# Gate logits from raw output rows, the norm's scale in the turned copy, two residual products for three, and a new step order

## The reference, cut to what matters

```python
x = L0_attn_x                                    # 4 x 1024 x 256, 4096 rows
x = x + 0.5 * ffn(layernorm(x))                  # 8 experts, capacity 160, top 1
x = x + attn(layernorm(x))
x = x + 0.5 * ffn(layernorm(x))

# attn, after the gated complex scan and the projection Wo:
y   = layer_norm(y + x, ln1_scale, ln1_bias)
h   = gelu(y @ W1 + b1)
out = layer_norm(h @ W2 + b2 + y, ln2_scale, ln2_bias)
# ffn: logits = tokens @ gate_w + gate_b, softmax, argmax, dispatch, two products, combine
```

## Time and profile before

| | us |
|---|---|
| median of 3 runs | 762.57 (762.26 to 764.51) |
| the profiled execution's own time | 763.36 |
| its span | 761.7 |
| first stage, to the first load of `attention` | 0 to 145.2 |
| `attention` | 145.2 to 650.6 |
| second expert stage | 650.6 to 761.7 |

### The profile page before, as it was taken

How to read it: one execution, slowest core, us unless ns; L and a number is a source line. 1 busy time by engine, 2 the same in 40 slices (tenths; PEclk the granted TensorE clock), 3 DMA queues, 4 the chain that set the end, 5 groups by cost and what they waited for, 6 DMA issues and landing times. The chain is left out here.

```text
span 761.7 us, 11459 instructions
## 1 busy us (share of the span) xinstructions
PE 638.8 (84%) x4229; PEld 571.8 (75%) x4229; DVE 465.7 (61%) x1012; ACT 465.5 (61%) x831; POOL 207.8 (27%) x321
## 2 busy tenths in 40 slices
PE   6848999175798999999999999899985995379995
PEld 3437999153577888789789889889885895379994
DVE  5663500235686888988988988978989542631000
ACT  3314443048767898897997988988876352134440
POOL 6140011210121425226235145142231331130112
PEclk9959999678779999999999999999999998579998
DMA  6996970330100201201301211011011130834720
GB/s 196 337 301 210 344 238 24 105 125 28 55 29 0 70 28 43 97 1 43 98 2 42 98 42 43 28 43 42 1 42 42 36 133 14 286 115 130 262 92 24
DMA packets 48816, 74.07 MB, mean 97 GB/s; under 512 B 4614, under 2 KB 40539, under 8 KB 48696
## 3 DMA queue, kind: packets, MB, share of 16 engines
q1 hardware_dynamic: 44408, 59.84, 23.8%
q0 software_dynamic: 4352, 13.49, 5.0%
HBM read 62.45 MB, written 15.20 MB: 102 GB/s over the span
## 5 line engine op out<-in xcount | busy, mean ns | idle before, releaser
L1531 PE MATMUL bank<-zt_h,w_in_h 128*128 128x512 f32 x192 | 82.3, 428 | 14.7 <-ACT kv L1439 6.8
L1531 PE MATMUL bank<-yt_h,w_h 128*128 128x256 f32 x256 | 77.3, 302 | 8.3 <-DVE yt_l L1333 4.9
L1533 PE MATMUL bank<-zt_h,w_in_l 128*128 128x512 f32 x192 | 78.9, 411 | 0.0
L1532 PE MATMUL bank<-zt_l,w_in_h 128*128 128x512 f32 x192 | 78.8, 410 | 0.0
L916 PE MATMUL bank<-xdt,ring 128*128 128x160 f32 x512 | 76.8, 310 | 1.6 <-ACT hid L773 0.6
L916 PEld LDWEIGHTS bank<-xdt,ring 128*128 128x128 f32 x512 | 74.2, 199 | 2.7 <-issue 1.8
L1531 PE MATMUL bank<-w_h,ht_h 128*128 128x256 f32 x256 | 74.6, 291 | 0.4 <-DVE ht_l L1340 0.4
L929 PE MATMUL bank<-hid,ring 128*128 128x160 f32 x512 | 72.5, 300 | 1.5 <-DVE idx_s L710 0.7
L1532 PE MATMUL bank<-yt_l,w_h 128*128 128x256 f32 x256 | 73.2, 286 | 0.0
L1533 PE MATMUL bank<-yt_h,w_l 128*128 128x256 f32 x256 | 72.9, 285 | 0.0
L737 DVE SCALAR_TENSOR_TENSOR xo<-bank,gate,xg 128x256 f32<-128x256 f32 x20 | 9.3, 482 | 103.8 <-PE bank L941 103.8
(11 more groups left out here) (245 smaller groups left out, 1600.6 us busy)
## 6 DMA issues: line engine op xcount, KB each, us to landing
ring<-in_L_ffn_w SPq DMA_DIRECT2D x32, 1024.0 KB, 7.8
xc<-in_L_attn_x SPq DMA_DIRECT2D x8, 512.0 KB, 4.3
zb<-x_mid SPq DMA_DIRECT2D x8, 512.0 KB, 4.9
z_mid<-zb POOLq DMA_DIRECT2D x8, 512.0 KB
zr<-z_mid SPq DMA_DIRECT2D x16, 256.0 KB, 2.8
xr<-x_mid SPq DMA_DIRECT2D x16, 256.0 KB
...
```

Source lines behind the costliest of these rows:

```text
L1531: T.matmul(out, left[0], right[0], start=start, stop=False)
L1532: T.matmul(out, left[0], right[1], start=False, stop=False)
L1533: return T.matmul(out, left[1], right[0], start=False, stop=stop)
```

## The change

`next_norm` goes: PE turns `xo` itself, the logits are made with `gate_c` (the router's weights less their mean over the 256 rows, which the first stage already makes), and DVE multiplies them by the row's reciprocal deviation when it reads them. POOL no longer makes the shift for it. `W1` is split unscaled; the norm's scale is applied when ACT and DVE read the turned copy, in two instructions of 256 columns each where one of 512 stood. The residual is then `yt_h` and `yt_l` times the identity, two products for three. The order is new: `FIRST_STEPS` is one period shorter and the loop over `STEPS` runs three times for two, `next_norm` is in no list, and steps are moved in all three. `LAST_STEPS` has the order of `STEPS`, run out to the end; its last lines are quoted below the diff.

```diff
-FIRST_FULL, LAST_FULL = 3, 5
-W1_PIECES = (6, 7)
+FIRST_FULL, LAST_FULL = 2, 5
...
 FIRST_STEPS = (
...
+    (0, "load_z", 0), (0, "z_stats", 0), (1, "load_z", 0), (2, "load_z", 0), (0, "z_norm", 0), (0, "z_turn", 0),
+    (0, "z_low", 0), (0, "project", 0), (0, "read", 0), (1, "z_stats", 0), (0, "project", 1), (0, "read", 1),
+    (0, "project", 2), (0, "read", 2), (0, "fold", 1), (0, "project", 3), (1, "z_norm", 0), (2, "z_stats", 0),
+    (0, "project", 4), (0, "read", 3), (0, "fold", 2), (0, "read", 4), (0, "fold", 4), (0, "square", 0),
+    (0, "size", 0), (0, "project", 5), (0, "read", 5), (0, "root", 0), (0, "gate_half", 0), (0, "fold", 5),
+    (1, "z_turn", 0), (0, "denominator", 0), (1, "z_low", 0), (1, "project", 0), (1, "project", 1),
+    (0, "inverse", 0), (0, "gate", 0), (3, "load_z", 0), (1, "read", 0), (0, "tangent", 0), (0, "tangent", 1),
...
 STEPS = (
...
+    (-2, "up", 5), (-1, "turned_back", 0), (1, "z_norm", 0), (0, "fold", 2), (0, "load_quarter", 0),
+    (-1, "scan", 0), (0, "project", 3), (-1, "scan", 1), (-2, "gelu", 4), (-2, "gelu", 5), (-2, "split", 4),
+    (-1, "rotate", 0), (-2, "next_turn", 0), (0, "read", 3), (-1, "back", 0), (-2, "split", 5), (-2, "up", 6),
+    (0, "project", 4), (-2, "up", 7), (-1, "gated", 0), (0, "read", 4), (0, "fold", 4), (-1, "gated", 1),
+    (-2, "gelu", 6), (-2, "logits", 0), (-1, "wo", 0), (0, "project", 5), (-2, "split", 6), (-2, "down", 1),
+    (-2, "gelu", 7), (-2, "split", 7), (-1, "mix_stats", 0), (0, "square", 0), (0, "read", 5), (0, "size", 0),
+    (0, "root", 0), (0, "denominator", 0), (-1, "mix_norm", 0), (0, "inverse", 0), (0, "fold", 5),
+    (-1, "mix_turn", 0), (0, "load_quarter", 1), (1, "z_turn", 0), (-2, "out_stats", 1), (-1, "wo", 1),
+    (-1, "mix_split", 0), (-1, "up", 0), (-1, "up", 1), (-2, "out_norm", 1), (1, "z_low", 0), (1, "project", 0),
+    (0, "tangent", 0), (0, "gate_half", 0), (0, "gate", 0), (-1, "gelu", 0), (-1, "gelu", 1), (-1, "split", 0),
+    (-1, "split", 1), (1, "read", 0), (-1, "up", 2), (-1, "up", 3), (0, "tangent", 1), (-1, "gelu", 2),
+    (-1, "split", 2), (-1, "gelu", 3), (2, "z_stats", 0), (-1, "split", 3), (1, "project", 1), (-1, "mix_stats", 1),
+    (0, "phase", 0), (1, "read", 1), (0, "rounding", 0), (-2, "next_turn", 1), (-1, "down", 0), (1, "fold", 1),
+    (-1, "mix_norm", 1), (-1, "mix_turn", 1), (0, "turns", 0), (-1, "out_stats", 0), (-1, "mix_split", 1),
+    (-2, "logits", 1), (3, "load_z", 0), (1, "project", 2), (1, "read", 2), (-1, "out_norm", 0), (-1, "up", 4),
 )
...
                 v.wait_ge(raw_in[n % RB], 16 * (n // RB + 1))
-                if n in W1_PIECES:
-                    raw = raw_view(n)
-                    for k in range(KD):
-                        ins = V.tensor_scalar(hi[:, k, :], raw[:, k, :], cst["ln1s"][:, k:k + 1], None, ALU.mult)
-                    ins.then_inc(raw_hi, 1)
-                    v.wait_ge(raw_hi, n + 1)
-                    for k in range(KD):
-                        ins = V.scalar_tensor_tensor(lo[:, k, :], raw[:, k, :], cst["ln1s"][:, k:k + 1],
-                                                     hi[:, k, :].bitcast(F32), ALU.mult, ALU.subtract)
-                    ins.then_inc(raw_done, 1)
-                    continue
                 V.tensor_copy(hi, raw_view(n)).then_inc(raw_hi, 1)
...
         xo = sb("xq", [P, QT, D])
-        x3 = sb("x3", [P, QT, D])
         x3t = sb("x3t", [P, KD, QW])
         b1_t = cst["b1"]
-        scale_f, scale_h = sb("scale_f", [P, KD, P]), sb("scale_h", [P, KD, P], F32R)
-        scale_l = sb("scale_l", [P, KD, P], F32R)
+        ident_r = sb("ident_r", [P, P], F32R)
         ln1b_raw = sb("ln1b_raw", [64, D])
...
                 pool.wait_ge(var[2], 2 * b.n + (q + 1))
-                power(cst["mean_rstd"][:, tiles(b, q), 1], cst["mean_rstd"][:, tiles(b, q), :], "eps_in", QT, rstd[2], shq[1])
+                power(cst["mean_rstd"][:, tiles(b, q), 1], cst["mean_rstd"][:, tiles(b, q), :], "eps_in", QT, rstd[2])
 
...
                     own.link(V.tensor_tensor(b2_raw[32:33, :], b2_raw[32:33, :], ln1b_raw[32:33, :], ALU.add))
-                    for k in range(KD):
-                        own.step(V.tensor_scalar(scale_f[:, k, :], ident[:], cst["ln1s"][:, k:k + 1], None, ALU.mult))
-                    own.after()
-                    own.link(V.tensor_copy(scale_h[:], scale_f[:]))
-                    own.step(V.tensor_tensor(scale_l[:], scale_f[:], scale_h[:].bitcast(F32), ALU.subtract))
+                    own.step(V.tensor_copy(ident_r[:], ident[:]))
                     own.step(V.tensor_copy(b2_hl[0:1, :], b2_raw[0:1, :]))
...
             def mix_split(b, q):
                 quarter_no = b.n * 2 + q
-                v.wait_ge(yf_ready, quarter_no + 1)
                 wait(v, down_ready, quarter_no)
-                V.tensor_tensor(yt_l[:], turn_n[:].rearrange("p (k n) -> p k n", k=KD), yt_h[q][:].bitcast(F32),
-                                ALU.subtract).then_inc(yt_ready, 1)
+                v.wait_ge(yf_ready, KD * (quarter_no + 1))
+                for k in range(KD):
+                    V.scalar_tensor_tensor(yt_l[:, k, :], turn_n[:, k * QW:(k + 1) * QW], cst["ln1s"][:, k:k + 1],
+                                           yt_h[q][:, k, :].bitcast(F32), ALU.mult, ALU.subtract).then_inc(yt_ready, 1)
 
             def split(b, j):
...
                 wait(v, o_stored, quarter_no * 16)
-                wait(v, x3_ready, quarter_no)
+                wait(v, x3t_ready, quarter_no)
                 for t in range(QT):
...
             def logits(b, q):
-                v.wait_ge(lgq_ready, b.n * 2 + (q + 1))
-                V.tensor_tensor(cst["logits"][:, bass.ds(b.n * JT + q * QT, QT), :],
-                                turn_x[:, 0:QT * NE].rearrange("p (t e) -> p t e", e=NE),
-                                cst["gate_b"][:].unsqueeze(1).to_broadcast([P, QT, NE]), ALU.add).then_inc(lgq_done, 1)
+                quarter_no = b.n * 2 + q
+                v.wait_ge(rstd[2], quarter_no + 1)
+                v.wait_ge(lgq_ready, quarter_no + 1)
+                for t in range(QT):
+                    no = b.n * JT + q * QT + t
+                    ins = V.scalar_tensor_tensor(cst["logits"][:, no, :], turn_x[:, t * NE:(t + 1) * NE],
+                                                 cst["mean_rstd"][:, no, 1:2], cst["gate_b"][:], ALU.mult, ALU.add)
+                    if t < QT - 1:
+                        own.step(ins)
+                ins.then_inc(lgq_done, 1)
 
...
             def mix_norm(b, q):
                 act.wait_ge(rstd[0], b.n * 2 + (q + 1))
-                norm_rows_act(vn, vn, rsq[0], shq[0], QT, n_ready)
-
-            def next_norm(b, q):
-                act.wait_ge(rstd[2], b.n * 2 + (q + 1))
-                wait(act, x3t_ready, b.n * 2 + q)
-                norm_rows_act(x3, xo, cst["mean_rstd"][:, tiles(b, q), 1], shq[1], QT, x3_ready)
+                norm_rows_act(vn, vn, rsq[0], shq, QT, n_ready)
 
             def z_turn(b, j):
...
                 wait(act, down_ready, quarter_no - 1)
-                S.activation(yt_h[q][:].rearrange("p k n -> p (k n)"), turn_n[:], ACT.Copy).then_inc(yf_ready, 1)
+                for k in range(KD):
+                    S.activation(yt_h[q][:, k, :], turn_n[:, k * QW:(k + 1) * QW], ACT.Copy,
+                                 scale=cst["ln1s"][:, k:k + 1]).then_inc(yf_ready, 1)
 
             def gelu(b, j):
...
 
-            run(act, dict(z_norm=z_norm, mix_norm=mix_norm, next_norm=next_norm, z_turn=z_turn, read=read, back=back, square=square, root=root, inverse=inverse, phase=phase, rounding=rounding, turns=whole,
+            run(act, dict(z_norm=z_norm, mix_norm=mix_norm, z_turn=z_turn, read=read, back=back, square=square, root=root, inverse=inverse, phase=phase, rounding=rounding, turns=whole,
                           gate_half=gate_half, mix_turn=mix_turn, gelu=gelu, next_turn=next_turn), own,
...
             def mix_turn(b, q):
...
                 pe.wait_ge(n_ready, quarter_no + 1)
-                wait(pe, yt_ready, quarter_no)
+                wait(pe, yt_ready, KD * quarter_no)
                 for k in range(KD):
...
             def up(b, j):
...
                 if m == 0:
-                    pe.wait_ge(yt_ready, b.n * 2 + (q + 1))
+                    pe.wait_ge(yt_ready, KD * (b.n * 2 + q + 1))
                 wait(pe, gelu_done[m % 2], b.n * 4 + (2 * q + m // 2))
...
                         part = o[:, k * P:(k + 1) * P]
-                        T.matmul(part, yt_h[q][:, k, c], scale_h[:, k, :], start=False, stop=False)
-                        T.matmul(part, yt_h[q][:, k, c], scale_l[:, k, :], start=False, stop=False)
-                        ins = T.matmul(part, yt_l[:, k, c], scale_h[:, k, :], start=False, stop=k == KD - 1)
+                        T.matmul(part, yt_h[q][:, k, c], ident_r[:], start=False, stop=False)
```

(25 more changed lines are left out.)

161 lines of the change are left out of this document (57 added, 104 removed).

## The result

The changed kernel takes **740.62 us** (median of 4 runs, 737.30 to 741.28) against 763.54 for the kernel before on the same chip: ratio 0.970, 95% interval 0.967 to 0.972. That is 22.9 us less; the forecast was 745.0, from 735 to 755. The profiled execution took 740.64 us with a span of 738.9.

What follows compares the result with a forecast made beforehand. PE was taken to bound the steady periods, DVE and ACT close behind, with cross-engine chains setting fill and drain. Terms 5.5 + 3.3 + 2.3 + 6.5 = 17.6 us off 763.36 gave 745.8, 745.0 against the median; range 735 to 755.

Steps and rivals of the forecast that it cites:

- The residual products: Two short PE products fewer in each of 32 tiles, 0.22 us a tile, 7.0 us over 16 quarters.
- The steady period: Between ends of first-quarter down in mid-attention: 52.4 us, 1.1 less each, -5.5 us over five periods.
- the two waits: PE waiting for DVE's second fold (qg) and for yo in each steady period, some 2.7 us together.
- The fill: Start of attention: milestones at 187.0, 215.8 and 247.6, earlier by 3.4, 2.0 and 4.4 us; mean taken, -3.3 us.
- The last full period: Block 6: yo sooner by 1.4 us and two shorter down worth 0.9, together -2.3 us.
- The drain: End of attention: earlier yo, shorter down, no next_norm ahead of gelu, last turn starting at once; -6.5 us.
- The last turn: At the drain's end PE's turn starts as soon as xo is whole, without waiting for statistics, POOL and ACT: -3.7 us.
- ACT and DVE costs: Two instructions for one: +0.3 us a quarter for ACT's copy of turned rows, +0.2 for DVE's mix_split.
- Rival 1: PE alone sets the pace: period 51.1 us, with best ends of the other terms 735.2 us; chance 0.17.
- Rival 2: The new order gives nothing; only work taken from the path counts, 7.0 + 3.7, giving 751.9 us; chance 0.22.
- Rival 3: PE's clock falls at the two new waits, 1.9 us a time, 22.8 us back: slower, 767.8 us; chance 0.06.

Runs made afterwards that it cites:

- the last kernel: Changed kernel with first-quarter out_norm later, Abs early, two buffers for output and x rows, PE's turns and logits a quarter later: 736.13 us, ratio 0.964 against the kernel before.
- the run with two row buffers: Changed kernel's arithmetic in exactly the order of the kernel before, without next_norm, with two output-row buffers for one: 763.79 us against 764.26 before.
- project 5: Changed kernel with PE's project part 5 put ahead of wo and DVE's fold part 4 ahead of gated: 762.6 us.
- the fold first: Changed kernel with DVE's second fold (of qg) put ahead of turned_back: 745.02 us.

## Why the prediction was right, point by point

- **Direction and size.** The terms came to 17.6 us and 22.7 were measured between the two profiled executions, 740.64 against 763.36. No term had the wrong sign; the fill, the periods and the last period were sized too small. Inside `attention` the gain is 26.3 us (7.6, 8.3, 3.8 and 6.6 in the table) and not 17.6. The 3.5 us lost ahead of it and behind it, which the prediction put at nothing, bring the total back towards the forecast, and that is luck.
- **The residual products.** 0.22 us a tile was right (timeline of after), and the kernel with the third product gave 6.6 us between spans and 5.7 between medians against 7.0. By an estimate from the Trainium skill (VectorE: DVE Perf Modes, section on the TRN2 errata) it would be 56 ns for each, 3.6 us in all. The trace has 0.11 us wherever the product before it is also short, and decides against that figure.
- **The steady period.** Forecast 52.4, measured 51.9. PE's own part was right, 33.2 us. DVE's was put at 19.1 and took 18.7. The walk started from 20.2 us of the kernel before, and these hold a wait for ACT that the new order has no longer:
```profile
419.39 1.23 DVE L1284 TENSOR_TENSOR t_a<-t_d,kv 128x1024 f32<-128x1024 f32 x1 [0.42 <-ACT t_d L1487]
```
  PE's work in the part was put at 16.4 (by its own rates the 8.4 and 5.6 in it are 8.3 and 5.8, with the same sum) and was 16.7 and 17.0 in turn. So the two waits were there, at the places named, with 2.1 and 1.4 us in turn in place of 2.7. Mis-sized: "the period is 52.4 us, 1.1 less"; it was 1.7 less.
- **The fill.** The walk gave 187.0, 215.8 and 247.6 and the trace has 187.1, 215.4 and 246.6. But `attention` began 2.2 us later than in the profile that the walk stood on, so the fill itself is 7.6 us shorter and not 4.4, and that the walk's times were met to a microsecond is luck. What the walk leaves out is the clock: it adds up durations of before, and in the fill the granted clock rose from 0.79 to 0.82, with PE busy 4.6 us less for eight products more. How much of the missing 3.2 us this makes no run separates. And taking "the mean, -3.3" was the wrong choice: only the last of the three milestones passes its gain on. The order makes all of the gain, 98.7 and 98.8 us with the old arithmetic.
- **The last full period.** -2.3 forecast, -3.8 measured: `yo` after 18.8 us in place of the 19.3 forecast, and from `yo` to `down` 28.7 us in place of before's 31.0, where only the two shorter `down` had been counted.
- **The drain.** -6.5 forecast, -6.6 measured to the last logits and -5.8 to the end of the stage (79.6 to 73.8 us), but by two errors. Block 7's `yo` was to come 0.8 sooner and came 0.3 later: DVE waits 1.0 us there for the scaled copy `yt_h`. What follows made up for it, with some 7 us less from `yo` to the last logits where 5.7 less were forecast; that the errors cancel is luck. The last turn is as predicted: it starts with `xo`, where PE waited 3.7 us in the earlier trace rows.
```profile
619.92 0.88 DVE L1330 SCALAR_TENSOR_TENSOR xq<-xq,rsq,xr 128x256 f32<-128x256 f32 x2 [0.23 <-DVE xq L1318]
...
620.85 1.12 PE L1595 MATMUL bank<-ident,xq 128*128 128x128 f32 x4 [3.16 <-DVE xq L1330]
```
- **ACT and DVE costs.** +0.24 and +0.18 us a quarter for the copy and the split, against +0.3 and +0.2.
- **Rival 1** (PE alone, 735.2) did not come: DVE sets 18.7 us of each block. (The 3.6 and 7.4 in its sum, for the last period and the drain, stand there without a working; 3.8 and 6.6 were measured.) Its time was all but reached by moving DVE's work, in the last kernel.
- **Rival 2** (the order gives nothing, 751.9) had it the wrong way round. The order alone gives 11 us, and it is the arithmetic that gives nothing alone. The prediction's sum added "7.0 + 3.7" as if taken from the path in any order; the run with two row buffers shows that in the old order it doesn't hold. Its sum was near because both came together.
- **Rival 3** (the clock falls at the waits) did not come in the changed kernel: its four middle waits for `yo`, 0.9 to 1.0 us, are followed by eight products of `wo` in 1.99 us, and the periods have clock 1.00. Its mechanism is real nonetheless. In the kernels with project 5 or the fold first, waits of 1.5 to 1.9 us are followed, if not each time, by stretches at the lower clock; their periods are 54.9 and 52.9 us. The Trainium skill (TensorE: Matmul & The Clock Gate, "A second HAM failure mode") says that frequent short idling alone can bring the low clock. The steady periods of after, with two waits each and clock 1.00, don't show it; two of the five of the kernel with the fold first do, with 0.97.
